# Selective scan, row steps: where VectorE takes the low half of x_dbl and where TensorE computes x_dbl

## The reference

```python
x_hw = xc.reshape(B, D, L); x_wh = xc.transpose(0, 1, 3, 2).reshape(B, D, L)
xs = jnp.stack([x_hw, x_wh, x_hw[..., ::-1], x_wh[..., ::-1]], axis=1)      # 4 directions
x_dbl = einsum('kcd,bkdl->bkcl', x_proj_w, xs)                              # 12 + 4 + 4 rows
dts, Bv, Cv = split(x_dbl, [12, 16], axis=2)
dt = softplus(einsum('kdr,bkrl->bkdl', dt_proj_w, dts) + dt_proj_b)
# for every direction, channel and state n of 4, along the positions t:
h[n] = exp(dt * A[n]) * h[n] + dt * B[n] * u
y    = sum over n of h[n] * C[n]                                           # + Ds * u
```

## Time and profile before

| | |
|---|---|
| runs | 9437.59 us median of 3 (9437.52 to 9439.44) |
| profiled execution, its own time | 9426.04 us |
| its span, first to last instruction | 9424.2 us |
| TensorE matmuls | 8659.1 us busy, 92% of the span |
| VectorE | 7371.5 us, 78% |
| ScalarE | 6096.1 us, 65% |
| GpSimd | 3293.4 us, 35% |
| mean granted TensorE clock | 0.975 of full speed |

### The profile page before, as it was taken

One profiled execution on the slowest core, in us unless ns is written; L12 is line 12 of the kernel. 1 busy time (PEld: TensorE's weight loads), 2 busy tenths in 40 slices (PEclk: granted clock), 3 DMA queues, 4 the chain that ended last, 5 costly groups with the idle time before them and its releaser, 6 DMA issues. The chain is left out here.

```text
span 9424.2 us, 104196 instructions
## 1 busy us (share of the span) xinstructions
PE 8659.1 (92%) x26436; PEld 4640.1 (49%) x26436; DVE 7371.5 (78%) x8225; ACT 6096.1 (65%) x7436; POOL 3293.4 (35%) x1874
## 2 busy tenths in 40 slices
PE   7899988999889998899988999889998899988999
PEld 3336733367333673336733367333673336633366
DVE  6987769876698766987679876798767987679876
ACT  6765667656675566755667556675566755677555
POOL 2860028600385003850038500385003850038500
PEclk9999999999999999999999999999999999999999
DMA  1320013200132001320013200132001320023200
GB/s 52 116 79 11 11 53 111 80 11 11 55 115 76 11 10 55 116 75 10 12 58 111 75 10 12 60 114 71 10 12 60 116 68 10 12 66 110 68 12 12
DMA packets 286693, 503.21 MB, mean 53 GB/s; under 512 B 142155, under 2 KB 143215, under 8 KB 253431
## 3 DMA queue, kind: packets, MB, share of 16 engines
q1 hardware_dynamic: 286199, 497.81, 17.7%
HBM read 467.99 MB, written 29.47 MB: 53 GB/s over the span
## 5 line engine op out<-in xcount | busy, mean ns | idle before, releaser
L1363 DVE TENSOR_TENSOR pl<-pf,ph 128x1024 fp32r<-128x1024 f32 x1024 | 1254.1, 1225 | 1014.2 <-ACT ph L1003 1008.0
L1217 DVE TENSOR_TENSOR_SCAN h<-ps,h,dbu 128x512 f32<-128x512 f32 x1536 | 1882.7, 1266 | 52.2 <-POOL dbu L1068 29.9
L1068 POOL TENSOR_TENSOR dbu<-bs,du 128x1024 f32<-128x1024 f32 x768 | 1808.5, 2370 | 54.1 <-POOL du L1059 54.1
L1003 ACT ACTIVATE ph<-pf 128x1024 fp32r<-128x1024 f32 x1024 | 1085.7, 1060 | 753.5 <-PE ps L695 753.2
L867 ACT ACTIVATE ps<-dt,negA 128x512 f32<-128x512 f32 x1536 | 1037.9, 687 | 720.4 <-DVE h L1217 720.1
L1023 POOL MEMSET sqb<- 64x512 f32 x16 | 8.3, 519 | 3985.4 <-issue 3980.4
L997 ACT ACTIVATE pf<-ps 128x1024 f32<-128x1024 f32 x1024 | 1051.0, 1026 | 534.9 <-PE ps L682 534.9
L1347 DVE TENSOR_REDUCE mx<-ps 128x1 f32<-128x512 f32 x1792 | 1167.9, 683 | 78.7 <-PE ps L600 60.5
L1225 DVE TENSOR_TENSOR hc<-h,ps 128x1024 f32<-128x1024 f32 x768 | 937.5, 1221 | 113.9 <-PE ps L481 20.0
L481 PE MATMUL ps<-xhl,selr 128*128 128x512 f32 x1536 | 756.2, 577 | 259.8 <-DVE hc L1225 259.5
L1053 POOL TENSOR_TENSOR dt<-dt,ze 128x1024 f32<-128x1024 f32 x256 | 604.5, 2361 | 1044.0 <-ACT dt L860 1043.9
(11 more groups left out here) (200 smaller groups left out, 14514.2 us busy)
## 6 DMA issues: line engine op xcount, KB each, us to landing
bs<-rows SPq DMA_DIRECT2D x256, 1024.0 KB, 5.2
bs<-rows SPq DMA_DIRECT2D x512, 256.0 KB, 6.1
xa<-in_x SPq DMA_DIRECT2D x130, 256.0 KB, 2.9
xb<-in_x SPq DMA_DIRECT2D x130, 128.0 KB, 3.0
out<-fa SPq DMA_DIRECT2D x64, 256.0 KB, 2.1
rdb<-rden SPq DMA_DIRECT2D x56, 192.0 KB, 3.6
out<-fa SPq DMA_DIRECT2D x64, 128.0 KB, 2.4
xhl<-ct SPq DMA_DIRECT2D x256, 8.0 KB
```

The source lines that it names most:

```text
L1003: A(ph[:, mp % 2, :, :], pf[:, mp % 2, :, :], ACT.Copy).then_inc(S["ph_ready"], 1)
L1068: pool.tensor_tensor(dbu[:, q, :, :], bs[par][:, q, :, :], du[:, r:r + 1, :].to_broadcast([P, 2, T]), ALU.mult).then_inc(S["dbu_ready"], 1)
L1217: dve.tensor_tensor_scan(h[:, j, ::step], ps[:, 2 + e, ::step], dbu[:, q, e, ::step], h[:, j, end:end + 1], ALU.mult, ALU.add)\
L1363: TT(pl[:, mp % 2, :, :], pf[:, mp % 2, :, :], ph[:, mp % 2, :, :].bitcast(F32), ALU.subtract)\
```

## The change

Three calls change their place; no instruction is added or removed, and only row steps are touched.

- VectorE: `low_half` of a chunk stood at the end of the step two ahead of it (`low_half(at + 2)` behind the third product). It now stands in the next step, as `low_half(at + 1)` between `scans` and `times_c` of the first pair.
- TensorE: `xdbl` for `after` stood first in the step. It now stands behind `sum_rest` and `spread(1)`, directly ahead of `dtproj`.
- ScalarE: `copy_xd` for `after` stood between the two decays of the second pair. It now stands behind them and `add_y1`, ahead of `decay` of the third pair.

```diff
@@ TensorE, body @@
-                    if after and at + 2 < EV:
-                        xdbl(*after, b * EV + (at + 2))
                     if before:
                         sum_rest(*before, g - 1)
                     spread(1, *now, at, g)
+                    if after and at + 2 < EV:
+                        xdbl(*after, b * EV + (at + 2))
                     if after:
                         dtproj(*after, at + 2, g + 2)
                     sum_first(*now, g)
@@ ScalarE, body @@
                     decay(k, 1, 0, s + 1, par, g)
-                    if after and at + 2 < EV:
-                        copy_xd(at + 2, g + 2)
                     decay(k, 1, 1, s + 1, par, g)
                     if before:
                         if at > EV:
                             add_y0(*before, g - 1)
                         add_y1(*before, g - 1)
+                    if after and at + 2 < EV:
+                        copy_xd(at + 2, g + 2)
                     decay(k, 2, 0, s + 2, par, g)
@@ VectorE, body @@
                         scans(now[0], q, s)
+                        if q == 0 and before and at + 1 < EV:
+                            low_half(at + 1)
                         times_c(q, s)
...
                     if after:
-                        if at + 2 < EV:
-                            low_half(at + 2)
                         residue(g + 2)
```

## The result

The changed kernel takes 9831.2 us, median of 4 runs (9826.4 to 9837.3), against 9437.6 before: a ratio of 1.0418 with a 95% interval of 1.0400 to 1.0436. It is 394 us slower. The forecast was 9770 in a range of 9685 to 9835, so the direction and the range held, the time near the upper end. The mean granted clock of TensorE fell from 0.975 to 0.949.

What follows compares the result with a forecast made beforehand. Row steps were taken as bound by a loop through ScalarE, as long as VectorE's work; per image 34.0 + 2.3 - 0.2 + 5.4 = 41.5 us, 332 in eight, on 9437.6 gave 9770 us, range 9685 to 9835.

Steps and rivals of the forecast that it cites:

- The loop through ScalarE: Row steps: chain from `dtproj` through ScalarE to the decays sets the period, 17.48 us with a store, 16.50 without.
- x_dbl and its copy: TensorE, ahead of `dtproj`: it starts 4.80 us after T0 (first pair's product with C) instead of 2.41, 2.39 later.
- SyncE's rows of B leave later: SyncE, rows of B for `after`: they leave later by the copy's delay, costed at nothing.
- The low half: VectorE, between recurrences and product: recurrences' start to T0 (first pair's product with C) takes 3.21 us, 0.63 more a period.
- Step 0, +2.3, and steps 14 and 15, -0.2: First and last steps of an image: +2.3 us (+1.2 to +3.5) and -0.2 us (-0.4 to +0.3).
- The sum at full clock: Whole kernel if no gap lets TensorE's clock fall: 9727 us.
- TensorE's clock: Gap ahead of `sum_rest`: clock falls in 0.8 of 8 storing periods, 0.4 of 5 others, 0.64 us each, 5.4 an image.
- The bound of 8.3 an image: Upper end for TensorE's clock falling in the row steps: 13 periods at 0.64 us each.
- VectorE as the bound: Rival, row steps: VectorE binds and the change only mends its order, 9379 to 9430 us, say 9420; 3 in 100.
- only the low half counting: Rival, row steps: x_dbl is hidden, storing periods get 0.63 us longer, 9478 us; 5 in 100.
- no fall of the clock: Rival, TensorE's gaps: none lets the clock fall, 9727 us; counted inside the forecast, which keeps 84 in 100.
- a clock that stays low through x_dbl and `dtproj`: Rival, TensorE: each takes 3.78 us instead of 1.98 in all 13 periods, about 10140 us; 5 in 100.

Runs made afterwards that it cites:

- E2: The changed kernel with TensorE's gap ahead of `sum_rest` filled by repeating `spread(0)`, five times in storing steps, three times in others: 9702.4 us, ratio 1.0280.
- E5: The changed kernel with the low half back at the end of the step and TensorE's gap filled by repeats of `spread(0)`: 9638.9 us, ratio 1.0219.
- E6: The changed kernel with `dtproj` reading the chunk before's copy of x_dbl (two buffers, another output) and TensorE's gap filled by repeats of `spread(0)`: 9578.1 us, ratio 1.0159.
- E1: The changed kernel with the low half back at the end of the step, x_dbl and its copy still moved: 9832.6 us, ratio 1.0417.
- E4: The changed kernel with `dtproj` on the chunk before's copy (two buffers, another output) and ahead of x_dbl, the copy behind `soft_exp`: 9575.2 us, ratio 1.0147.

## Why the prediction was right, and which size was off

- **The loop through ScalarE, with no slack in storing steps**: right. `dtproj` waits for the copy, ScalarE has no pause to the decays, and at full clock (E2) the periods are those worked out, less 0.23.
- **x_dbl and its copy, 2.39 us later**: right in place, a little large. At full clock `dtproj` starts at T0 + 0.05 + 1.22 + 3.30 = 4.57, 2.16 later; x_dbl follows `spread(1)` by 0.58 (1473.23 to 1473.81), not by 0.73, and `dtproj` follows x_dbl by 2.72, not 2.80. E5 shows the two moves alone: 207 us at full clock. With `dtproj` on the older copy (E6 against E2) 119 us go, so the wait for the copy is nearly half of the 265 us that the change costs at full clock. What is left beside it and the low half, 265 - 119 - 58 = 88 us, is put down to x_dbl's own time ahead of `dtproj`; no run tests that by itself. That SyncE's rows of B leave later cost nothing, as was assumed: in the 13 periods of the second image VectorE's recurrences waited for ScalarE's decays alone, 32.4 us in 30 waits.
- **The low half, 0.63 a period**: right at full clock (E2 against E5: 0.60). Its saving on VectorE is there too, 0.04 instead of 0.12 ahead of the product, and worth nothing, since VectorE is no longer the bound.
- **Step 0, +2.3, and steps 14 and 15, -0.2**: measured +0.87 and -0.40 in the second image. Over all eight it is +1.8 and -0.2 in the mean, since step 0 of the kernel before took 16.3 in three images and 17.5 to 17.8 in five.
- **The sum at full clock**: 9727 was worked out; E2 has 9702.
- **TensorE's clock: the term that was mis-sized.** The prediction's step was "I take 0.8 of the 8 storing periods and 0.4 of the 5 others", at 0.64 us a fallen period: 43 us in all, 66 at most. The changed kernel loses 129 us against E2. In the second image the 13 periods have 235.41 - 219.38 = 16.0 us more, 1.23 each. Both factors were low. The clock fell in all 13 (in 102 of 104 over the eight images), also behind gaps of 2.41 us, where the trace before had shown five falls in eight at 2.47. And a fall cost more than the 0.41 for a later `spread(1)` and the 0.23 for a slow one. It can be read at `dtproj`, which E2 starts at T0 + 4.57: in nine of the 13 periods the changed kernel starts it at T0 + 5.38 to 5.48, in the other four at T0 + 6.6. These delays add up to 16 us, which is the whole loss. The four are those in which `spread(1)` came 4.50 behind the start of `sum_rest`, where the prediction had 3.74, and x_dbl followed `spread(1)` by 1.45 (298.43 to 299.88 is such a one), where the prediction had 0.96. The bound of 8.3 an image was a bound on the count only; the price was one reading at another step.
- **The range held with some luck.** The clock's +86 us and the -25 of the other terms make the 61 us between 9770 and 9831. Had the sum at full clock been exact, 9727 + 129 = 9856 would have come out, above the range's 9835.
- **By the Trainium skill** ("TensorE: Matmul & The Clock Gate", HAM oscillation), a loop whose wait for a DMA lets the clock fall in each turn pays for the slow restart in each turn. This trace agrees, for waits on ScalarE of 2.42 to 3.40 us: 14 steps of 14 in the second image.
- **The rivals**: VectorE as the bound falls with its share of 78%; only the low half counting falls with E1; no fall of the clock is E2's time and not the kernel's; a clock that stays low through x_dbl and `dtproj` isn't seen, both run at full rate (1.02 for two matmuls, 1.98 for four) in the rows after.

Open is why the restart takes 3.94, 4.50 or 3.5 us in turn, and so whether the mean of 1.23 us that it costs a period would hold for another length of step.

## What to carry to other kernels

Before an instruction is moved to fill a wait of the busiest engine, follow the loop from one step to the next through all engines: an engine busy for 96% can share the bound with a chain that is busy nowhere, and a producer moved directly ahead of its consumer puts its own time and each hand-over between engines into that chain. A longer step also opens gaps on TensorE, and the price of its clock comes on top; filling the gap with repeated work separates the two in one run. Costs of parts that feed the same wait don't add: the low half was worth 58 us with the clock kept and none with the clock falling.

## What the runs showed of the hardware that was not expected

- How long TensorE had stood still ahead of `sum_rest` doesn't by itself tell whether half the clock follows. Behind 2.41 to 2.44 us it followed each time in the changed kernel, but not in step 1 of three images of E1; behind 2.47 to 2.49 us in the kernel before in five of eight images. At 2.08 to 2.17 us (E4) both occurred. Behind 1.80 to 1.83 us it never followed in the kernel before (five images), but in E1's step 15 in five of eight, and at 1.70 to 1.73 us (step 9 of E4) in two of eight. Behind the 1.41 to 1.61 us of E2 and E6 it never did.
- The clock can fall after work has begun again: in step 3 of the second image of the changed kernel, behind a pause of 2.43 us, the first two matmuls of `sum_rest` took 1.12, as at the full rate, and the four others 3.51 instead of E2's 1.88.
- The changed kernel became 129 us faster when TensorE did one `spread` three or five times instead of once in its row steps.
